# Latent attention: six key tiles transposed on TensorE in two groups of three, ten regrouped over DRAM

## Chip, cores and metric

One core of one Trainium2 chip runs the whole program. The metric is the device time of one execution in microseconds; less is better. Before the change it is 2612.72 us, the median of 3 runs (2611.89 to 2612.78).

## The reference

Four blocks follow one another on a [2048 tokens x 128] float32 array: a state-space block, a local-attention transformer, a latent attention, and a mixture of experts, with a layer norm between them. The change touches the third alone:

```python
h = layernorm(x) * ln_scale + ln_bias
c_q, c_kv = h @ w_down_q.T, h @ w_down_kv.T          # 64 latent channels each
q = rope(c_q @ w_up_q.T); k = rope(c_kv @ w_up_k.T)  # 16 heads of 64
v = c_kv @ w_up_v.T
attn = softmax(q @ k.T / 8)                          # 2048 x 2048 per head
out = (attn @ v) @ w_out.T + x
```

Attention isn't masked, so every head has 2048 x 2048 probabilities.

## The kernel before

**Tiling.** A unit of work is one head and one chunk of 512 queries; there are 64 of them (UNITS). Heads go in pairs (w = 0 and 1), and a pair of units (w = 0, then w = 1, on the same chunk j) is the period that repeats 32 times. A unit has four iterations, r = 0 to 3, one for each 128 queries; G = 4U + r counts them, 256 in all. The 2048 keys are 16 tiles of 128 (T).

**An iteration.** TensorE (L1597 to L1622) computes the scores of the *next* iteration, G + 1, into four PSUM banks of 512 keys (score_banks, L1377), banks 0 and 1 once the first half of the exponentials of G has left them, banks 2 and 3 after the second half. VectorE takes the row maximum of each bank and then of the four (row_max, L1407 to L1414). ScalarE turns the scores into probabilities in two halves of 1024 keys (exps, L1416 to L1422), into probs[:, slot] in SBUF, queries on partitions.

The product with the values needs keys on partitions, so the probabilities have to be turned, and this is done in two ways:

- Key tiles 0 to NEAR - 1 = 7 go through TensorE: turn_tiles (L1398) transposes four tiles of 128x128 into the one PSUM bank `turned`, and ScalarE copies the bank into `near` (copy_tiles, L1403). This happens twice in an iteration: group A (tiles 0 to 3) after the scores, then a stretch of the mix, then group B (tiles 4 to 7). ScalarE's order is copy A, both exps, copy B.
- Key tiles 8 to 15 (FAR = 8) go over DRAM: VectorE transposes 32x32 blocks of probs (turn_blocks, L1474 to L1480, 128x1024) into `blocks[:, r % 2]`, SP writes them to `bounce` in DRAM (write_blocks, L1482) and reads them back regrouped into `far[:, w]` (read_blocks, L1487).

turn_blocks(G) waits for the write of G - 2, which used the same half of `blocks` (L1477). It comes in VectorE's order after row_max(G + 1) and before row_max(G + 2); with r = 3 two small instructions for the softmax sums (reciprocals, L1466) stand between.

**The mix** of a unit's probabilities with the values (mix, L1424) comes one unit of the same head later, in pieces of four tiles: MIXED_AT (L1515) has tiles 4 to 7 in r = 0, 8 to 11 in r = 1, 12 to 15 in r = 2, and 0 to 3 of the other head's unit in r = 3. Before the first piece with a far tile TensorE waits until that head's four reads have landed (L1608). The first mixed result goes through the output matmuls in r = 0 (output, L1442). In the units with w = 0, r = 1 and r = 3 also project the next pair's queries and keys (pieces, L1384).

**SP's queue** is one list in a fixed order (L1524 to L1546). For a unit: wait for the head's earlier reads; write 0; (w = 1: send_keys, four transfers); write 1; wait for mix_done, which the mix of r = 2 sets (L1533), since `far[:, w]` is free only then; read 0; read 1; write 2; read 2, which waits for write 2 to land (L1488); write 3; (w = 0: send_keys); send_q, two transfers; read 3, which waits for write 3 to land. Then the next unit's write 0.

POOL adds outputs to the accumulator and makes the rotated keys and queries of the next pair (make_parts, L1492). It and SP are otherwise not touched.

Of the kernel before, what the change touches and what calls it, by code (L numbers as in the profile page):

```python
# [9 lines left out]
ACT = mybir.ActivationFunctionType  # L10
AX = mybir.AxisListType

P = 128
D = 128
S = 2048
T = S // P
CH = 512
# [1099 lines left out]
HEADS_G, HEAD_G, LATENT = 16, 64, 64  # L1117
# [3 lines left out]
RT = 4  # L1121
QH = QW // 2
HALVES = S // QH
NEAR = 8
FAR = T - NEAR
RUN = FAR * 32


def latent_attention(nc, dram, const, x, acc):

    ident = const["ident"]
    spare = x[:].rearrange("p t d -> p (t d)")
    values = spare[:, 0:T * LATENT].rearrange("p (t c) -> p t c", c=LATENT)
    raw = spare[:, T * LATENT:2 * T * LATENT].rearrange("p (k n) -> p k n", k=2)
    with Space(nc, "g") as sp:
        c = sp.sb("c", [P, S])
        waves = sp.sb("waves", [P, HALVES, 2, QH])
# [3 lines left out]
        with Space(nc, "ga") as s:  # L1141
            norm = s.sb("norm", [P, 2])
            w_down = s.sb("w_down", [P, 2 * LATENT])
            w_v = s.sb("w_v", [P, PAIRS_G, LATENT])
            w_o = s.sb("w_o", [P, PAIRS_G, D])
            hT = s.sb("hT", [P, S])
            turned = s.ps("turned", [P, 2, CH])
            down = s.ps("down", [P, 2, CH])
            v_ps = s.ps("v_ps", [P, 2, CH])
            m_ps = s.ps("m_ps", [P, 2, CH])  # L1150
            m = {n: s.sem(n) for n in ("loaded", "turn_done", "hT_ready", "down_done", "c_ready", "v_done", "m_done",
                                       "doubled", "copied")}
            with nc.Block() as block:

                @block.sync
                def _(sync):
                    for d, n in ((norm, "g_norm"), (w_down, "w_down"), (w_v, "w_v"), (w_o, "w_o")):
                        sync.dma_start(d[:], dram[n]).then_inc(m["loaded"], 16)
                    sync.dma_start(waves[:], dram["g_waves"]).then_inc(waves_loaded, 16)

                @block.tensor
                def _(pe):
                    for g in range(NC):
                        if g >= 2:
                            pe.wait_ge(m["hT_ready"], g - 1)
                        for k in range(4):
                            ins = nc.tensor.transpose(turned[:, g % 2, k * P:(k + 1) * P], acc[:, 4 * g + k], ident[:])
                        ins.then_inc(m["turn_done"], 1)
                    pe.wait_ge(m["loaded"], 4 * 16)
                    for c_ in range(NC):  # L1170
                        pe.wait_ge(m["hT_ready"], c_ + 1)
                        if c_ >= 2:
                            pe.wait_ge(m["c_ready"], c_ - 1)
                        nc.tensor.matmul(down[:, c_ % 2], w_down[:], hT[:, c_ * CH:(c_ + 1) * CH], start=True,
                                         stop=True).then_inc(m["down_done"], 1)
                    for t in range(T):
                        ins = nc.tensor.matmul(v_ps[:, t // 8, (t % 8) * LATENT:(t % 8 + 1) * LATENT],
                                               hT[:, t * P:(t + 1) * P], w_down[:, LATENT:], start=True, stop=True)
                    ins.then_inc(m["v_done"], 1)
                    for k in range(2):  # L1180
                        if k:
                            pe.wait_ge(m["copied"], 2)
                        for h in range(8 * k, 8 * k + 8):
                            rows = slice(h % 2 * 64, h % 2 * 64 + 64)
                            at = h // 2 % 4
                            for half in range(2):
                                ins = nc.tensor.matmul(m_ps[half * 64:half * 64 + 64, h % 2, at * P:(at + 1) * P],
                                                       w_v[rows, h // 2], w_o[rows, h // 2], start=True, stop=True)
                        ins.then_inc(m["m_done"], 1)

                @block.vector
                def _(dve):
                    dve.wait_ge(m["loaded"], 4 * 16)
                    for g in range(NC):
                        dve.wait_ge(m["turn_done"], g + 1)
                        nc.vector.tensor_scalar(hT[:, g * CH:(g + 1) * CH], turned[:, g % 2], norm[:, 0:1],
                                                norm[:, 1:2], ALU.mult, ALU.add).then_inc(m["hT_ready"], 1)

                    dve.wait_ge(m["turn_done"], NC)
                    nc.vector.tensor_scalar(acc[:], x[:], 2.0, None, ALU.mult).then_inc(m["doubled"], 1)  # L1200
                    for c_ in range(NC):
                        cols = slice(c_ * CH, (c_ + 1) * CH)
                        dve.wait_ge(m["down_done"], c_ + 1)
                        nc.vector.tensor_scalar(c[0:64, cols], down[0:64, c_ % 2], 0.125, None, ALU.mult)
                        nc.vector.tensor_copy(c[64:P, cols], down[64:P, c_ % 2]).then_inc(m["c_ready"], 1)
                    dve.wait_ge(m["v_done"], 1)
                    dve.wait_ge(m["doubled"], 1)
                    nc.vector.tensor_copy(values[:, 0:NEAR].rearrange("p t c -> p (t c)"), v_ps[:, 0])
                    nc.vector.tensor_copy(raw[:, 0], v_ps[:, 1])
                    by_head = mixers[:, 2:].rearrange("p (g h) n -> p h g n", h=2)  # L1210
                    for k in range(2):
                        dve.wait_ge(m["m_done"], k + 1)
                        for h in range(2):
                            nc.vector.tensor_copy(by_head[:, h, 4 * k:4 * k + 4],
                                                  m_ps[:, h].rearrange("p (g n) -> p g n", n=D)).then_inc(m["copied"], 1)

                @block.gpsimd
                def _(pool):
                    nc.gpsimd.memset(mixers[:, 0:2], 0.0)
# [6 lines left out]
        probs = sp.sb("probs", [P, 2, S])  # L1226
        near = sp.sb("near", [P, 2, NEAR, QW])
        far = sp.sb("far", [P, 2, RT * 4, FAR, 32])
# [10 lines left out]
        turned = sp.ps("turned", [P, CH])  # L1239
# [42 lines left out]
        with nc.Block() as block:  # L1282

            @block.sync
            def _(sync):
                load_w(sync, 0, 0)
                load_w(sync, 1, 1)
                for k in range(4):
                    sync.dma_start(values[k:P:4, NEAR:].rearrange("p t c -> p (t c)"), raw[32 * k:32 * k + 32, 0])\
                        .then_inc(m["values_set"], 16)  # L1290
                sync.wait_ge(m["values_set"], 64)
                sync.wait_ge(m["zeroed"], 1)
# [105 lines left out]
        def turn_tiles(pe, r, tiles):  # L1398
            for k, t in enumerate(tiles):
                ins = nc.tensor.transpose(turned[:, k * P:(k + 1) * P], probs[:, r % 2, t * P:(t + 1) * P], ident[:])  # L1400
            ins.then_inc(m["turn_done"], 1)

        def copy_tiles(act, w, r, tiles):  # L1403
            nc.scalar.activation(near[:, w, tiles, r * P:(r + 1) * P], turned[:].rearrange("p (t n) -> p t n", n=P),  # L1404
                                 ACT.Copy).then_inc(m["near_copied"], 1)

        def row_max(dve, slot, before):  # L1407

# [108 lines left out]
        with nc.Block() as block:  # L1517
# [55 lines left out]
            def _(pe):  # L1573
# [4 lines left out]
                with pe.Fori(0, PAIRS_G // 2) as i:  # L1578
                    for turn in range(2):
                        g = 2 * i + turn  # L1580
                        for j in range(NC):
                            for w in range(2):
                                U = 8 * g + 2 * j + w
                                for r in range(RT):
# [14 lines left out]
                                    pe.wait_ge(m["exp_done"], 2 * G + 2)  # L1599
                                    score_banks(pe, (2, 3), q, k_of)  # L1600
                                    pe.wait_ge(m["near_copied"], 2 * G + 1)
                                    turn_tiles(pe, r, range(0, 4))
                                    if r == 0:
                                        pe.wait_ge(m["piece_taken"], 2 * (8 * g + 2 * j) + (4 if w else 1))
                                        pe.wait_ge(m["mixed_ready"], U + 1)
                                        slot = 2 * (2 * i + turn + (j + 2 + w) // NC) + 1 - w
                                        output(pe, mixers[:, bass.ds(slot, 1)].rearrange("p a n -> p (a n)"))
                                    if r == 1:  # L1608
                                        pe.wait_ge(landed[w], 64 * (4 * g + j + 1))
                                    if r == 3:  # L1610
                                        pe.wait_ge(m["mixed_ready"], U + 2)
                                        pe.wait_ge(m["near_copied"], 8 * U + 1)
                                    mix(pe, w if r < 3 else 1 - w, MIXED_AT[r])
                                    pe.wait_ge(m["near_copied"], 2 * G + 2)
                                    turn_tiles(pe, r, range(4, 8))
                                    if w == 0 and r == 1:
                                        pe.wait_ge(w_loaded[1 - turn], 16 * (i + 1 + turn))
                                        pe.wait_ge(m["out_taken"], U + 1)
# [39 lines left out]
            def _(act):  # L1658
# [4 lines left out]
                with act.Fori(0, PAIRS_G // 2) as i:  # L1663
                    for turn in range(2):
                        g = 2 * i + turn
                        for j in range(NC):
                            for w in range(2):
                                U = 8 * g + 2 * j + w
                                H = 8 * g + 2 * j
                                for r in range(RT):  # L1670
# [12 lines left out]
                                            take_piece(act, H, 1)  # L1683
                                        act.wait_ge(m["recip_ready"], U + 3)
                                    act.wait_ge(m["turn_done"], 2 * G + 1)
                                    copy_tiles(act, w, r, slice(0, 4))
                                    act.wait_ge(m["blocks_turned"], G + 1)
                                    exps(act, (r + 1) % 2, w if r < RT - 1 else 1 - w, (r + 1) % RT, G + 2)
                                    if r == 0:
                                        act.wait_ge(m["near_read"], 2 * U + 2)  # L1690
                                    act.wait_ge(m["turn_done"], 2 * G + 2)
                                    copy_tiles(act, w, r, slice(4, 8))
                take_output(act, UNITS)
                take_mixed(act, UNITS + 1)
                take_output(act, UNITS + 1)
# [359 lines left out]
```

## Time and profile before

| what | value |
|---|---|
| time, median of 3 runs | 2612.72 us |
| the profiled execution's own time | 2612.52 us |
| its span | 2610.7 us |
| PE / PEld busy | 2243.0 us (86%) / 1316.3 us (50%) |
| DVE / ACT / POOL busy | 1667.3 us (64%) / 1356.4 us (52%) / 851.6 us (33%) |
| DMA moved | 350.10 MB, mean 134 GB/s |
| mean granted TensorE clock | 0.926 of full speed |

PE is TensorE's matmuls and PEld its weight loads, DVE is VectorE, ACT is ScalarE, POOL is GpSimd, SP issues transfers. The span runs from the first to the last instruction; the time of the execution has 1.8 us more around it. The main loop of the latent attention lies between about 1000 and 2391 us of the span. A line of the timeline gives start, duration, engine, line, operation, output and inputs, how many instructions are merged in it, and in brackets how long the engine sat idle before it and what released it. SPq marks transfers as SP issues them: their duration there is the issuing, not the transfer.

### The profile page before, as it was taken

What the parts mean: (1) busy time and instruction counts of PE and PEld (TensorE: products, weight loads), DVE (VectorE), ACT (ScalarE), POOL (GpSimd) and SP (SyncE); (2) the same over time, 40 slices, a digit from 0 to 9 for tenths busy, and PEclk for the clock granted to TensorE, in tenths of its full rate; (3) what the DMA queues carried; (4) which work ended last, traced back from release to release, by engine and by line L of the source; (5) the groups of instructions that cost most, each with busy time, mean ns of one, the idle gap of its engine ahead of it and who ended that gap; (6) DMA issues with size and microseconds to landing.
All of it is one profiled execution on the core that took longest, in us unless ns stands there. A gap on an engine that the chain in (4) does not pass through costs nothing. (4 is left out here: it accounts for less than half of the span.)

```text
span 2610.7 us, 38329 instructions
## 1 busy us (share of the span) xinstructions
PE 2243.0 (86%) x11694; PEld 1316.3 (50%) x11694; DVE 1667.3 (64%) x3060; ACT 1356.4 (52%) x2757; POOL 851.6 (33%) x868
## 2 busy tenths in 40 slices
PE   4737989389895548999999999999999999998297
PEld 2522358343484324555555555555555555554144
DVE  5863566435664556777767777677777677774544
ACT  4222345123453105777767777677777677775121
POOL 0712333113332023434344434344434344443000
PEclk8978989689898768999999999999999999999598
DMA  1002000000000045777767677767676777675000
GB/s 30 1 1 100 1 1 2 19 25 1 1 2 8 12 150 157 237 237 228 238 210 234 226 236 231 233 226 234 228 234 227 228 232 237 228 234 186 33 1 17
DMA packets 229184, 350.10 MB, mean 134 GB/s; under 512 B 21460, under 2 KB 173908, under 8 KB 228564
## 3 DMA queue, kind: packets, MB, share of 16 engines
q1 hardware_dynamic: 228948, 347.32, 40.8%
q8 instruction: 103, 1.69, 0.3%
q14 instruction: 133, 1.09, 0.1%
HBM read 151.96 MB, written 136.31 MB: 110 GB/s over the span
## 5 line engine op out<-in xcount | busy, mean ns | idle before, releaser
L1411 DVE TENSOR_REDUCE g.most<-g_score 128x1 f32<-128x512 f32 x1028 | 638.7, 683 | 341.9 <-PE g_score L1381 341.8
L1419 ACT ACTIVATE g.probs<-g_score,g.bias 128x1024 f32<-128x1024 f32 x514 | 568.1, 1110 | 69.6 <-DVE g.bias L1414 58.6
L1381 PE MATMUL g_score<-g.keys,g.q_unit 128*128 128x512 f32 x2056 | 560.6, 412 | 28.9 <-issue 12.5
L1404 ACT ACTIVATE g.near<-g_turned 128x512 f32<-128x512 f32 x512 | 305.4, 596 | 325.0 <-PE g_turned L1400 325.0
L1381 PEld LDWEIGHTS g_score<-g.keys,g.q_unit 128*128 128x128 f32 x2056 | 360.5, 190 | 148.7 <-ACT g.probs L1419 63.3
L1400 PEld LDWEIGHTS g_turned<-top.ident,g.probs 128*128 128x128 f32 x2048 | 234.2, 140 | 243.1 <-issue 208.1
L1478 DVE STREAM_TRANSPOSE g.blocks<-g.probs 128x1024 f32<-128x1024 f32 x256 | 318.8, 1245 | 37.2 <-DMA bounce<-g.blocks 24.3
L1400 PE MATMUL g_turned<-top.ident,g.probs 128*128 128x128 f32 x2048 | 321.7, 280 | 0.0
L1432 PE MATMUL g_mix_ps<-g.near,mid.y_tok 128*64 128x512 f32 x1056 | 258.8, 612 | 5.7 <-DMA g.far<-bounce 5.7
L1432 PE MATMUL g_mix_ps<-g.far,mid.y_tok 128*64 128x512 f32 x1056 | 255.2, 605 | 0.0
L1498 POOL TENSOR_TENSOR mid.y_tok<-mid.y_tok,g.waves 128x512 f32<-128x512 f32 x128 | 163.6, 1278 | 227.7 <-ACT mid.y_tok L1396 227.7
L1460 POOL TENSOR_TENSOR g.scaled<-g.scaled,g.recip 128x512 f32<-128x512 f32 x67 | 69.7, 1040 | 423.8 <-ACT g.scaled L1452 412.6
L1432 PEld LDWEIGHTS g_mix_ps<-g.near,mid.y_tok 128*64 128x64 f32 x1056 | 64.9, 138 | 104.1 <-issue 96.4
L1432 PEld LDWEIGHTS g_mix_ps<-g.far,mid.y_tok 128*64 128x64 f32 x1056 | 64.3, 136 | 99.8 <-issue 99.8
L1419 ACT ACTIVATION_READ_ACCUMULATOR g.probs<-g_score,g.bias 128x1 f32 x514 | 100.6, 196 | 0.0
L1501 POOL TENSOR_TENSOR mid.y_tok<-mid.y_tok 128x256 f32<-128x256 f32 x128 | 93.1, 727 | 10.1
L1509 POOL TENSOR_TENSOR g.k_part<-mid.y_tok,g.zero 128x256 fp32r<-128x256 f32 x64 | 39.2, 612 | 168.3 <-DMA g.keys<-g.k_part 163.0
L1464 POOL TENSOR_TENSOR top.x_tok<-top.x_tok,g.scaled 128x512 f32<-128x512 f32 x67 | 85.6, 1277 | 5.2
L728 POOL TENSOR_TENSOR la1.qkT<-lp1.rotated,lp1.turned_by 128x512 f32<-128x512 f32 x32 | 40.6, 1269 | 128.0 <-DVE lp1.turned_by L704 128.0
L728 POOL TENSOR_TENSOR la0.qkT<-lp0.rotated,lp0.turned_by 128x512 f32<-128x512 f32 x32 | 40.6, 1269 | 125.3 <-DVE lp0.turned_by L704 125.3
L1396 ACT ACTIVATE mid.y_tok<-g_side 128x512 f32<-128x512 f32 x128 | 77.4, 604 | 1.8
L1444 PE MATMUL g_side<-g.mixers,g.mixed 128*128 (+1 forms) x536 | 71.8, 278 | 1.2 <-ACT g.mixed L1440 1.2
(352 smaller groups left out, 3290.3 us busy)
## 6 DMA issues: line engine op xcount, KB each, us to landing
bounce<-g.blocks SPq DMA_DIRECT2D x256, 512.0 KB, 6.1
g.far<-bounce SPq DMA_DIRECT2D x256, 512.0 KB
g.q_unit<-g.q_pair SPq DMA_DIRECT2D x132, 256.0 KB, 4.7
g.keys<-g.k_part SPq DMA_DIRECT2D x256, 64.0 KB, 3.6
g.far<-g.near SPq DMA_DIRECT2D x8, 512.0 KB
lt.cos<-cos SPq DMA_DIRECT2D x1, 2048.0 KB, 8.1
lt.sin<-sin SPq DMA_DIRECT2D x1, 2048.0 KB, 12.2
g.waves<-g_waves SPq DMA_DIRECT2D x1, 2048.0 KB, 9.7
```

What stands on the lines that cost most here:

```text
L728: nc.gpsimd.tensor_tensor(qkT[:, f, cols(c)], rotated[:, n % 2], turned_by[:, n % 2], ALU.add)\
L1381: ins = nc.tensor.matmul(score[:, b], q[:, part], k_of(b), start=(part == 0), stop=(part == 1))
L1396: nc.scalar.activation(raw[:, kind], side[:, kind], ACT.Copy).then_inc(m["piece_taken"], 1)
L1400: ins = nc.tensor.transpose(turned[:, k * P:(k + 1) * P], probs[:, r % 2, t * P:(t + 1) * P], ident[:])
L1404: nc.scalar.activation(near[:, w, tiles, r * P:(r + 1) * P], turned[:].rearrange("p (t n) -> p t n", n=P), ACT.Copy).then_inc(m["near_copi ...
L1411: nc.vector.tensor_reduce(most[:, slot, k:k + 1], score[:, k], AX.X, ALU.max, negate=True)\
L1419: nc.scalar.activation(probs[:, slot, k * 2 * CH:(k + 1) * 2 * CH], score[:, 2 * k:2 * k + 2].rearrange("p b n -> p (b n)"), ACT.Exp, bias ...
L1432: ins = nc.tensor.matmul(out, values[:, t], moving, start=(t < 2), stop=(t >= T - 2))
L1464: nc.gpsimd.tensor_tensor(a, a, scaled[:], ALU.add).then_inc(m["added"], 1)
L1478: nc.vector.transpose(blocks[:, r % 2].rearrange("p j t c -> p t j c"), probs[:, r % 2, NEAR * P:].rearrange("p (t j a) -> p t j a", j=4, ...
L1498: nc.gpsimd.tensor_tensor(both, both, waves[:, at].rearrange("p s n -> p (s n)"), ALU.mult)\
L1501: nc.gpsimd.tensor_tensor(total, total, both[:, QH:], ALU.add).then_inc(m["order"], 1)
```

## The change

NEAR goes from 8 to 6, so FAR from 8 to 10. Group A is tiles 0 to 2 and group B tiles 3 to 5; the copy out of the PSUM bank has 384 columns. turn_blocks works on 128x1280, each write and read of `bounce` carries 640 KB for 512 KB, and a read's contiguous pieces (RUN * 4 bytes) are 1280 bytes for 1024, a write's 5120 for 4096. Tiles 6 and 7 are now far, and they are mixed in r = 0; the wait for the reads moves there from r = 1. The values of the ten far tiles are staged in one contiguous area by one copy more.

```diff
-NEAR = 8
+NEAR = 6
+TURN = NEAR // 2
 FAR = T - NEAR
 RUN = FAR * 32
...
+    spread_values = spare[:, T * LATENT:T * LATENT + FAR * LATENT]
...
-                    nc.vector.tensor_copy(values[:, 0:NEAR].rearrange("p t c -> p (t c)"), v_ps[:, 0])
-                    nc.vector.tensor_copy(raw[:, 0], v_ps[:, 1])
+                    nc.vector.tensor_copy(values[:, 0:NEAR].rearrange("p t c -> p (t c)"), v_ps[:, 0, 0:NEAR * LATENT])
+                    nc.vector.tensor_copy(spread_values[:, 0:CH - NEAR * LATENT], v_ps[:, 0, NEAR * LATENT:])
+                    nc.vector.tensor_copy(spread_values[:, CH - NEAR * LATENT:], v_ps[:, 1])
...
-                    sync.dma_start(values[k:P:4, NEAR:].rearrange("p t c -> p (t c)"), raw[32 * k:32 * k + 32, 0])\
+                    sync.dma_start(values[k:P:4, NEAR:].rearrange("p t c -> p (t c)"), spread_values[32 * k:32 * k + 32])\
...
-            nc.scalar.activation(near[:, w, tiles, r * P:(r + 1) * P], turned[:].rearrange("p (t n) -> p t n", n=P),
-                                 ACT.Copy).then_inc(m["near_copied"], 1)
+            nc.scalar.activation(near[:, w, tiles, r * P:(r + 1) * P],
+                                 turned[:, 0:TURN * P].rearrange("p (t n) -> p t n", n=P), ACT.Copy).then_inc(m["near_copied"], 1)
...
-                                    turn_tiles(pe, r, range(0, 4))
+                                    turn_tiles(pe, r, range(0, TURN))
                                     if r == 0:
...
                                         output(pe, mixers[:, bass.ds(slot, 1)].rearrange("p a n -> p (a n)"))
-                                    if r == 1:
                                         pe.wait_ge(landed[w], 64 * (4 * g + j + 1))
...
-                                    turn_tiles(pe, r, range(4, 8))
+                                    turn_tiles(pe, r, range(TURN, NEAR))
...
-                                    copy_tiles(act, w, r, slice(0, 4))
+                                    copy_tiles(act, w, r, slice(0, TURN))
...
-                                    copy_tiles(act, w, r, slice(4, 8))
+                                    copy_tiles(act, w, r, slice(TURN, NEAR))
```

## Rows read from the trace of the kernel before

**Rows 1.** Busy time by stretch; then waits, 1000 to 2400 (total us, times, longest).

```profile
core 0: us, PE busy (x) PEld busy (x) DVE busy (x) ACT busy (x) POOL busy (x), PEclk, DMA share, GB/s
1400.00:1500.00 100.00, 100.00 (x526) 59.14 (x523) 72.71 (x120) 73.79 (x133) 43.24 (x50) 1.00 0.70 232
...
DVE g.blocks L1478 <- DMA bounce<-g.blocks: 24.3, 30, 2.2
```

**Rows 2.** Groups of instructions, 1000 to 2400: count, busy us, mean ns, idle before.

```profile
L1400 PE MATMUL g_turned<-top.ident,g.probs 128*128 128x128 f32 x2044 | 321.1, 280 | 0.0
L1478 DVE STREAM_TRANSPOSE g.blocks<-g.probs 128x1024 f32<-128x1024 f32 x256 | 318.8, 1245 | 37.2 <-DMA bounce<-g.blocks 24.3 <-issue 4.5 <-ACT g.probs L1419 1.2
...
L1432 PE MATMUL g_mix_ps<-g.far,mid.y_tok 128*64 128x512 f32 x1040 | 251.6, 605 | 0.0
L1432 PE MATMUL g_mix_ps<-g.near,mid.y_tok 128*64 128x512 f32 x1032 | 249.9, 605 | 0.0
```

**Rows 3.** Timeline of PE, 1735 to 1785: the scores that open an iteration.

```profile
1739.17 2.25 PE L1381 MATMUL g_score<-g.keys,g.q_unit 128*128 128x512 f32 x8
1744.96 2.09 PE L1381 MATMUL g_score<-g.keys,g.q_unit 128*128 128x512 f32 x8
1750.94 2.12 PE L1381 MATMUL g_score<-g.keys,g.q_unit 128*128 128x512 f32 x8
1755.71 2.25 PE L1381 MATMUL g_score<-g.keys,g.q_unit 128*128 128x512 f32 x8
1761.84 2.11 PE L1381 MATMUL g_score<-g.keys,g.q_unit 128*128 128x512 f32 x8
1767.50 2.09 PE L1381 MATMUL g_score<-g.keys,g.q_unit 128*128 128x512 f32 x8
1772.24 2.25 PE L1381 MATMUL g_score<-g.keys,g.q_unit 128*128 128x512 f32 x8
1777.14 2.09 PE L1381 MATMUL g_score<-g.keys,g.q_unit 128*128 128x512 f32 x8
```

**Rows 4.** Timeline, 1766 to 1778: the rest of the iteration from 1767.50.

```profile
1768.23 2.48 DVE L1411 TENSOR_REDUCE g.most<-g_score 128x1 f32<-128x512 f32 x4 [1.66 <-PE g_score L1381]
...
1769.43 0.60 PE L1400 MATMUL g_turned<-top.ident,g.probs 128*128 128x128 f32 x4
...
1770.75 0.16 DVE L1414 TENSOR_REDUCE g.bias<-g.most 128x1 f32<-128x4 f32 x1
...
1770.94 1.11 ACT L1419 ACTIVATE g.probs<-g_score,g.bias 128x1024 f32<-128x1024 f32 x1 [0.28 <-DVE g.bias L1414]
...
1771.82 0.66 PE L1400 MATMUL g_turned<-top.ident,g.probs 128*128 128x128 f32 x4
```

**Rows 5.** SP's issues in a unit with w = 0, 1748 to 1790; then VectorE.

```profile
1755.50 0.93 SPq L1489 DMA_DIRECT2D g.far<-bounce  x2
1756.57 0.41 SPq L1484 DMA_DIRECT2D bounce<-g.blocks  x1
1762.83 0.36 SPq L1489 DMA_DIRECT2D g.far<-bounce  x1
1763.30 0.44 SPq L1484 DMA_DIRECT2D bounce<-g.blocks  x1
...
1768.43 0.66 SPq L1489 DMA_DIRECT2D g.far<-bounce  x1
1769.21 1.41 SPq L1484 DMA_DIRECT2D bounce<-g.blocks  x1
...
1776.15 1.25 DVE L1478 STREAM_TRANSPOSE g.blocks<-g.probs 128x1024 f32<-128x1024 f32 x1 [0.50 <-DMA bounce<-g.blocks]
```

**Rows 6.** Busy time by stretch: reads 0 and 1 moving, then write 2.

```profile
1758.00:1759.50 1.50, 1.50 (x10) 0.64 (x10) 1.09 (x4) 1.11 (x3) 1.25 (x1) 1.00 1.00 289
1760.00:1761.50 1.50, 1.50 (x12) 1.10 (x12) 0.74 (x1) 1.50 (x5) 1.26 (x3) 1.00 1.06 407
```

**Rows 7.** Timelines of DVE and PE, 2250 to 2270: the same wait, longest.

```profile
2255.99 1.25 DVE L1478 STREAM_TRANSPOSE g.blocks<-g.probs 128x1024 f32<-128x1024 f32 x1 [2.15 <-DMA bounce<-g.blocks]
...
2261.40 2.29 PE L1381 MATMUL g_score<-g.keys,g.q_unit 128*128 128x512 f32 x8 [1.09 <-ACT g.probs L1419]
```

## The prediction

> **What bounds the kernel now.** I read the busy time by stretch first. In the main loop TensorE is busy all the time at full granted clock, VectorE and ScalarE 73% and 74%, and the DMA engines 70% at 232 GB/s [rows 1]. By this alone TensorE is the limit, and taking work from it pays in full. The starts of the scores show that this holds in half of the iterations only [rows 3]. From one start to the next a pair of units has 5.79 (w = 0, r = 0), 5.98, 4.77, 6.13 (r = 1, 2, 3), 5.66, 4.74, 4.90 (w = 1, r = 0, 1, 2), and an r = 3 that is bare like the last two. Four are long: they hold the output matmuls or the projected pieces. Four are bare.
>
> A bare one is bound twice [rows 3, 4]. TensorE fills it, but there is also a loop through three engines: scores start at 1767.50, the first maximum 0.73 later (1768.23), four maxima take 2.48, the bias ends at 1770.91, the first half of the exponentials runs from 1770.94 to 1772.05, and the next scores start at 1772.24. That is 4.74 us with no gap over 0.3. TensorE's work in a bare iteration could vanish, and it would still take 4.74. The long ones have about an engine-microsecond to spare against this loop.
>
> Then the waits. The only stall by a transfer is VectorE's block transposition for the write two iterations before it: 30 times, 24.3 us in total, 0.81 on average [rows 1]. Rows 5 show where: in r = 2 of w = 1, once a pair. Its write (write 0 of w = 1) is issued at 1769.21, VectorE is ready at 1775.65, and starts at 1776.15 when it has landed, 6.9 after its issue. SP issued it that late because its queue is a chain: the mix of r = 2 (w = 0) and group B end before the scores of 1755.71 [rows 3], the mix itself at about 1755.3; reads 0 and 1 at 1755.50, write 2 at 1756.57, read 2 at 1762.83 when write 2 has landed, write 3 at 1763.30, read 3 at 1768.43 when write 3 has landed, write 0 at 1769.21 [rows 5]. The chain takes 20.9 us, VectorE is ready after 20.35. It is balanced to half a microsecond against compute, and the change lengthens it.
>
> **TensorE's part.** Two of eight transposes go. A group of four occupies 0.60 (A) and 0.66 (B) with a last one of 0.28 [rows 2, 4], so one more costs (0.60 - 0.28)/3 = 0.107 and (0.66 - 0.28)/3 = 0.127, together 0.234 an iteration. In the four long iterations that counts: 0.94. In the bare ones only what lies over the loop's 4.74: 4.77 and 4.90 give 0.03 and 0.15 less a rounding, 0.17. Sum 1.11 a pair, 32 pairs: **-35.5 us**. Bounds: 256 x 0.234 = 60 if the loop were no limit, 30 if only the long ones gain.
>
> **ScalarE's part.** Two copies an iteration lose a quarter of their columns. ScalarE is 26% idle [rows 1] and the copies stand before or after the exponentials, not in them, so I count nothing. If they were in the loop they would make it shorter, hence the 60 above.
>
> **VectorE's part.** The transposition goes from 1024 to 1280 columns: 1.245 us [rows 2] to 1.51 if some of it is fixed, 1.56 in proportion. It sits between the bias and the next maximum. In the tight place the bias ends at 1775.65 and the next maximum could start 0.73 after the scores of 1777.14, at 1777.87 [rows 3 to 5]: 2.22, less 1.25 and about 0.2 for the reciprocals, so a wait of about 0.8 is free there. The longest wait, 2.15, left TensorE idle for 1.09 and so had 0.8 to 1.06 free [rows 7]. With the longer transposition (0.27) and the loop at 4.75 for 4.90 (0.15) 0.4 is left. In itself the transposition costs nothing: VectorE's idle time covers it.
>
> **The mix.** Far and near matmuls take the same, 605 ns [rows 2], so tiles 6 and 7 cost the same from `far`. The wait for the reads comes one iteration earlier. Read 3 of a w = 0 unit goes out at 1768.43 [rows 5], the r = 0 mix that now needs it begins after 1782, the end of this pair [rows 3]. Even if it lands 2 us later than now there are some 6 us left: nothing, with the DMA queue backed up at most a few us.
>
> **The transfers.** Each of the 512 grows by 131 KB. The rates when the engines are full are 289 GB/s while reads move and 407 GB/s while a write does [rows 6], so +0.45 for a read and +0.32 for a write if all of it scales with bytes; if a read's packets have a fixed part, +0.3. In the chain from the end of the mix to the landing of write 0 stand reads 0 and 1 and write 2, read 2 and write 3, read 3 and write 0, each batch awaited: 4 x 0.45 + 3 x 0.32 = 2.8, or 7 x 0.3 = 2.1. I take 2.4, nearer the middle since the share is 1.00 to 1.06 in both stretches (the engines, not the issuing, are the limit), with a part of write 3's growth hidden by SP's own issuing of keys and queries. Lower bound 0 for the reads if their time is set by the count of packets, which stays: then 1.0. Page "DMA: Bandwidth & Descriptors" of the Trainium skill, section "Anatomy of one DMA", fits 2.0 us plus bytes / 436 GB/s (for another issuing path); by this estimate a transfer grows by 0.30 and the chain by 2.1, and the total below would come to 2650. This trace's reads are slower than that rate.
>
> At the same time compute gets to the place sooner: the mix of r = 2 ends 0.11 earlier in its iteration, but the long iterations r = 3 and r = 0 lose 0.23 each: VectorE is ready 20.0 after it for 20.35, 0.36 sooner.
>
> New wait: 0.7 now + 2.4 + 0.36 = 3.45 a pair, of which 0.4 is free, so 3.05 stall the loop of three engines. Nothing makes this good afterwards, as TensorE has no backlog. Today about 0.25 a pair is lost there (an average wait of 0.81 with 0.8 free, and a few long ones). Net 2.75. At the three back edges of the loop over pairs TensorE stands still anyway, so 29 pairs: **+80 us**. The opening copies, the larger fills and the last read that ends the stage: **+2**.
>
> Sum: -35.5 + 80 + 2 = +46 on the profiled execution's 2612.5, which is the median within 0.2: **2658 us**.
>
> **Rivals.**
> *A, the forecast: write 0 of w = 1 becomes the limit.* With growths of 2.1 to 2.8, 2648 to 2671; with doubts on the free part 2635 to 2685. For: 30 waits stand there already, in nearly every pair. Chance 0.64.
> *B, same place, cheap transfers.* If the chain grows by under 1.1, the stall is under 1.75 and gain and loss cancel: growth 1.0 gives 2616, growth 0 gives 2590. It decides at a growth of 0.8. Against: share 1.00 at only 289 GB/s. Chance 0.16.
> *C, faster: the wait doesn't bind.* Should SP's chain shrink elsewhere (issues of 0.66 and 1.41 at its end are partly the queue's backlog, and they might overlap the landing), the wait stays free, and TensorE's saving counts: 2612.5 - 36 = 2577; with a shorter loop too, 2553. "Perfetto Trace Analysis" of the Trainium skill, section "Identifying the Most-Contended Engine", says to optimise first the engine with the highest occupancy, here TensorE; by that rule it is this case. The busy share speaks for it, the 4.74 loop and the waits against. It needs a chain that grows by next to nothing, since the free 0.4 is less than today's wait. Chance 0.13.
> *D, worse: more places wait.* The engines' share goes from 0.70 to about 0.84. If writes 2 and 3 come late for the next unit's r = 0 and r = 1 too, or the reads for the mix, a second stall of 1 to 2 us a pair adds 30 to 60: 2690 to 2720. Chance 0.07.
> That the change does not do what it says would show in the counts; nothing in it is conditional.
>
> **Chances and range.** About 0.2% (5 us) is what a measurement of this kernel tells from no change. Faster: C and half of B, 0.21. Same: the other half of B, 0.08. Slower: 0.71. A's own range is 2635 to 2685. For 8 in 10 the range has to take in B and the lower end of D: 2586 to 2694.
>
> **What would show it.** Right: L1400 has 1536 matmuls; the block transposition takes 1.5 us; read 2 is issued 7.1 to 7.5 after write 2 instead of 6.3; VectorE waits about 3.4 us for `bounce` in some 30 places, 100 us in all, in r = 2 of w = 1; that bare r = 3 iteration grows to 7.5 to 8; long iterations are 0.23 shorter, the other bare ones 4.75; DMA share about 0.8. Wrong: a DVE wait total under 40 us (B or C), bare iterations under 4.7 (the loop was no limit), or idle time of TensorE before the mix of r = 0 (D).

## The result, and the profile after

The changed kernel takes **2765.85 us** (2761.06 to 2771.67, 4 runs) against 2612.3 us (2608.01 to 2612.78) of the kernel before: ratio 1.0593, 95% interval 1.0564 to 1.0621. It is slower by 153 us. The forecast said slower by 46, with 2694 as its upper end.

The page, with the lines that answer to [rows 1, 2], first whole-span busy times, then the costliest groups (line engine op, out<-in, shapes, count | busy, mean ns | idle before, releaser):

```profile
span 2759.6 us, 37306 instructions
PE 2274.7 (82%) x11182; PEld 1312.4 (48%) x11182; DVE 1735.8 (63%) x3061; ACT 1296.9 (47%) x2757; POOL 850.1 (31%) x868
...
L1481 DVE STREAM_TRANSPOSE g.blocks<-g.probs 128x1280 f32<-128x1280 f32 x256 | 387.0, 1512 | 203.4 <-DMA bounce<-g.blocks 187.1
...
L1403 PE MATMUL g_turned<-top.ident,g.probs 128*128 128x128 f32 x1536 | 273.2, 288 | 22.4 <-ACT g.near L1407 22.4
```

The work did what was foreseen: 1536 transposes for 2048, VectorE's transposition 1.512 us. The time went into a wait: VectorE for the writes to `bounce`, 187.1 us for 24.3 [rows 1]. Who waited for whom (total us, times, longest), 1000 to 2550:

```profile
DVE g.blocks L1481 <- DMA bounce<-g.blocks: 187.1, 91, 5.3
...
ACT g.near L1407 <- DVE g.recip L1475: 71.7, 26, 3.7
...
PE g_score L1384 <- DMA g.keys<-g.k_part: 29.9, 8, 5.0
```

The second line is new, and the third as good as new (0.2 us before). With r = 3, ScalarE waits for the reciprocals before copy A, and those now stand behind the late transposition; and TensorE waits 8 times for the keys of the next pair of heads, whose transfers come behind write 0 in SP's queue.

The same place as in [rows 5], SP's issues of one unit with w = 0, and VectorE at its end:

```profile
1835.59 2.22 SPq L1492 DMA_DIRECT2D g.far<-bounce  x2
1837.94 0.41 SPq L1487 DMA_DIRECT2D bounce<-g.blocks  x1
1845.30 0.36 SPq L1492 DMA_DIRECT2D g.far<-bounce  x1
1845.77 0.44 SPq L1487 DMA_DIRECT2D bounce<-g.blocks  x1
...
1851.73 0.43 SPq L1492 DMA_DIRECT2D g.far<-bounce  x1
1852.29 1.62 SPq L1487 DMA_DIRECT2D bounce<-g.blocks  x1
...
1860.28 1.51 DVE L1481 STREAM_TRANSPOSE g.blocks<-g.probs 128x1280 f32<-128x1280 f32 x1 [4.41 <-DMA bounce<-g.blocks]
```

From read 0 to VectorE's start on the landing of write 0 it is 24.7 us, for 20.65 (1755.50 to 1776.15). Link by link against [rows 5]: reads 0 and 1 to write 2, 2.35 for 1.07 (SP itself takes 2.22 to issue the two reads, for 0.93); landing of write 2, 7.36 for 6.26; of write 3, 5.96 for 5.13; read 3 to write 0, 0.56 for 0.78; landing of write 0, 7.99 for 6.94. This unit lies above the mean: over 31 pairs the way from read 0 to VectorE's start takes 24.31 us on average for 20.85, and VectorE is ready for it after 20.08 for 20.16.

What TensorE makes of it, the starts of the scores as in [rows 3]:

```profile
1851.98 2.29 PE L1384 MATMUL g_score<-g.keys,g.q_unit 128*128 128x512 f32 x8
1857.17 2.31 PE L1384 MATMUL g_score<-g.keys,g.q_unit 128*128 128x512 f32 x8 [0.23 <-ACT g.probs L1422]
1865.96 3.63 PE L1384 MATMUL g_score<-g.keys,g.q_unit 128*128 128x512 f32 x8 [2.71 <-ACT g.probs L1422]
1872.92 2.10 PE L1384 MATMUL g_score<-g.keys,g.q_unit 128*128 128x512 f32 x8
```

r = 3 of w = 1 takes 8.79 us (1857.17 to 1865.96), and the next iteration, which doesn't wait for any transfer, 6.96. Its scores take 3.63 us for 2.10. Busy time by stretch says why (PE, PEld, DVE, ACT, POOL, granted clock, DMA share, GB/s):

```profile
1857.20:1866.00 8.80, 5.05 (x23) 2.54 (x23) 5.63 (x9) 3.67 (x8) 3.27 (x4) 0.99 0.89 288
1865.90:1869.40 3.50, 3.44 (x8) 2.73 (x9) 2.15 (x4) 1.49 (x4) 0.00 (x0) 0.51 0.70 269
```

TensorE was busy for 5.05 of 8.80 us, and then the granted clock is 0.51, the lower of its two levels (1.2 of 2.4 GHz).

The account over 31 pairs, from the starts of the scores, mean us before and after:

| iteration | before | after | forecast |
|---|---|---|---|
| w = 0: r = 1, 2, 3 | 5.98, 4.77, 6.14 | 5.76, 4.74, 6.00 | 5.75, 4.75, 5.90 |
| w = 1: r = 0, 1 | 5.66, 4.74 | 5.45, 4.72 | 5.43, 4.75 |
| w = 1: r = 2 | 4.93 | 5.89 | 4.75 |
| w = 1: r = 3 | 5.40 | 8.50 | 7.97 |
| w = 0: r = 0 (next pair) | 5.96 | 6.98 | 5.72 |

(The last two hold the three back edges of the loop in both kernels, so their forecast is the value before plus 80/31, and the value before less 0.23.) The 31 pairs take 1489.2 us for 1350.9, 138 more; the start and the last units another 11 (span less the pairs, 1270.4 for 1259.8). That is the profiled execution, 2761.43 us.

### The profile page after: what moved, and what is told of

It reads as the page before. It is cut to its first block and busy times, and to the rows that moved or that the text cites. A ratio compares the mean times of both kernels' runs of the same rounds, so it can differ in the third digit from the quotient of the medians.

```text
span 2759.6 us, 37306 instructions
## 1 busy us (share of the span) xinstructions
PE 2274.7 (82%) x11182; PEld 1312.4 (48%) x11182; DVE 1735.8 (63%) x3061; ACT 1296.9 (47%) x2757; POOL 850.1 (31%) x868
## 5 line engine op out<-in xcount | busy, mean ns | idle before, releaser
L1384 PE MATMUL g_score<-g.keys,g.q_unit 128*128 128x512 f32 x2056 | 607.3, 438 | 125.9 <-ACT g.probs L1422 73.9
L1384 PEld LDWEIGHTS g_score<-g.keys,g.q_unit 128*128 128x128 f32 x2056 | 388.7, 203 | 273.4 <-ACT g.probs L1422 146.4
L1481 DVE STREAM_TRANSPOSE g.blocks<-g.probs 128x1280 f32<-128x1280 f32 x256 | 387.0, 1512 | 203.4 <-DMA bounce<-g.blocks 187.1
L1407 ACT ACTIVATE g.near<-g_turned 128x384 f32<-128x384 f32 x512 | 250.9, 490 | 435.2 <-PE g_turned L1403 362.9
L1435 PE MATMUL g_mix_ps<-g.far,mid.y_tok 128*64 128x512 f32 x1320 | 322.7, 602 | 0.0
L1403 PEld LDWEIGHTS g_turned<-top.ident,g.probs 128*128 128x128 f32 x1536 | 185.5, 144 | 270.8 <-issue 193.5
L1403 PE MATMUL g_turned<-top.ident,g.probs 128*128 128x128 f32 x1536 | 273.2, 288 | 22.4 <-ACT g.near L1407 22.4
L1435 PE MATMUL g_mix_ps<-g.near,mid.y_tok 128*64 128x512 f32 x792 | 204.8, 625 | 6.2 <-DMA g.far<-bounce 6.2
L1435 PEld LDWEIGHTS g_mix_ps<-g.far,mid.y_tok 128*64 128x64 f32 x1320 | 83.4, 136 | 136.7 <-issue 136.7
L1435 PEld LDWEIGHTS g_mix_ps<-g.near,mid.y_tok 128*64 128x64 f32 x792 | 46.9, 140 | 69.5 <-issue 61.9
```

What stands on the lines that cost most here:

```text
L1384: ins = nc.tensor.matmul(score[:, b], q[:, part], k_of(b), start=(part == 0), stop=(part == 1))
L1435: ins = nc.tensor.matmul(out, values[:, t], moving, start=(t < 2), stop=(t >= T - 2))
L1481: nc.vector.transpose(blocks[:, r % 2].rearrange("p j t c -> p t j c"), probs[:, r % 2, NEAR * P:].rearrange("p (t j a) -> p t j a", j=4, ...
```

## The experiments

A line number in a trace's row is that of the run's own kernel. Each ratio is to the kernel before as it ran beside that experiment: 2612.87 us for 1 to 4, 2613.3 for 5 to 8, 2616.7 for 9 to 11.

**1. The bytes taken back.** All instructions of the change, with 512 KB a transfer: the last 256 of each partition's 1280 elements aren't moved, so two far tiles hold stale numbers.

```diff
-                           blocks[:, r % 2].rearrange("p j t c -> p (j t c)")).then_inc(written[r % 2], 16)
+                           blocks[:, r % 2].rearrange("p j t c -> p (j t c)")[:, 0:4 * SHORT]).then_inc(written[r % 2], 16)
...
-            sync.dma_start(far[:, w, 4 * r:4 * r + 4].rearrange("p i t c -> p i (t c)"),
+            sync.dma_start(far[:, w, 4 * r:4 * r + 4, 0:8].rearrange("p i t c -> p i (t c)"),
```

> The changed kernel, but every write and read of bounce carries 512 KB as before (the last 256 of each partition's 1280 elements stay behind, so two of the ten far tiles keep stale numbers). All its instructions stay. Theory (the extra bytes in SP's chain are the whole loss): 2612.5 - 36 = about 2577 (2570 to 2585), the DVE wait for bounce falls from 187 us to under 40, iterations r = 3 (w = 1) and r = 0 (w = 0) go from 8.8 and 7.0 to 4.8 and 5.6. Rival (the longer transposition on VectorE, or the wait for the reads moved to r = 0, is part of the loss): over 2600, with a wait for bounce that is small but r = 3 still over 6.

Measured 2597.93 us (2593.16 to 2604.04), ratio 0.9935 (0.9918 to 0.9951). The bytes are worth 2766 - 2598 = **168 us**, more than the whole loss, and the rest of the change, longer transposition and earlier wait for the reads among it, is a gain of 15. It isn't the 36 expected: the time lies between the expected range and the rival's. The wait doesn't vanish:

```profile
DVE g.blocks L1482 <- DMA bounce<-g.blocks: 36.3, 34, 4.2
```

That is my own sum: with the same chain, VectorE is ready 0.36 us sooner and has 0.4 free for 0.8, so the wait of 0.7 grows to 1.06 and 0.66 of it stalls, 29 x 0.66 = 19 us less the 7 lost before, 12. The trace has r = 3 of w = 1 at 5.80 us for 5.40, 12 us in 31 pairs. The expectation had left this out; the prediction had it. The other 9 us stay open.

**2. ScalarE's second wait.** The wait for the reciprocals moved behind copy A.

```diff
                                             take_piece(act, H, 1)
-                                        act.wait_ge(m["recip_ready"], U + 3)
                                     act.wait_ge(m["turn_done"], 2 * G + 1)
                                     copy_tiles(act, w, r, slice(0, TURN))
+                                    if r == 3:
+                                        act.wait_ge(m["recip_ready"], U + 3)
```

> The changed kernel, but ScalarE waits for the reciprocals in r = 3 after copy A instead of before it. The changed kernel's trace shows ScalarE waiting 72 us there, 26 times, since the reciprocals stand behind the late block transposition on VectorE. Theory (the exponentials still wait for the maxima behind the same transposition, so copy A has time): ScalarE's wait for the reciprocals disappears, the time stays within 6 us of the changed kernel's 2766, at most 15 less. Rival (this second coupling adds to the stall): 40 to 70 us less.

Measured 2782.47 us (2774.74 to 2794.61), ratio 1.0663 (1.0635 to 1.0690), above the range of both. The wait is gone from the trace, and nothing is gained; the rival is out. That it is some 17 us slower wasn't expected; the trace shows more waiting for `bounce` (204.6 us up to 2400), but why stays open.

**3. TensorE kept busy.** 8 extra transposes of the identity before group B and 20 after it, w = 1, r = 3 only.

```diff
+                                    if w == 1 and r == 3:
+                                        pe.wait_ge(m["piece_taken"], 2 * (8 * g + 2 * j) + 5)
+                                        filler(pe, 8)
                                     pe.wait_ge(m["near_copied"], 2 * G + 2)
                                     turn_tiles(pe, r, range(TURN, NEAR))
+                                    if w == 1 and r == 3:
+                                        filler(pe, 20)
```

> The changed kernel, with 28 extra transposes of a constant tile into a free half bank in r = 3 of w = 1, 8 before group B and 20 after it, about 3 us of TensorE work in its idle time there. Theory (after some 3 us of idling TensorE is granted the lower clock, and the next scores take 3.6 us for 2.1): scores in r = 0 of w = 0 take 2.1 to 2.3 again and that iteration goes from 7.0 to 5.5, 27 pairs x 1.5 = 40 us less, 2726 (2715 to 2745). Rival (the long scores come from something else, such as the load of the transfers): no gain, and up to 20 us more from the extra work.

Measured 2800.59 us (2796.83 to 2803.16), ratio 1.0715 (1.0697 to 1.0733): 35 more, not 40 less. The mechanism did what the theory said: r = 0 of w = 0 went from 6.98 to 5.55 us on average. But what VectorE waits for `bounce` rose, and the waits are in other iterations now:

```profile
1847.71 1.51 DVE L1485 STREAM_TRANSPOSE g.blocks<-g.probs 128x1280 f32<-128x1280 f32 x1 [3.25 <-DMA bounce<-g.blocks]
1854.19 1.51 DVE L1485 STREAM_TRANSPOSE g.blocks<-g.probs 128x1280 f32<-128x1280 f32 x1 [2.41 <-DMA bounce<-g.blocks]
```

These are r = 1 and r = 2 of a unit with w = 0; all waits of VectorE for `bounce` come to 265.1 us up to 2400. On average over 31 pairs r = 2 and 3 of w = 0 went from 4.74 and 6.00 to 5.14 and 7.18 us, r = 0 of w = 1 from 5.45 to 5.89. I read this as a row of awaited transfers that closes on itself: write 0 lands, VectorE transposes, write 2 goes out, lands, read 2, write 3, read 3, the next unit's write 0. At 640 KB it limits the units with w = 0 too, as soon as compute gets through them quicker. r = 3 of w = 1 grew as well, from 8.50 to 9.03, though VectorE's wait at its place hardly did (138.8 us in all for 135.7); why stays open. Whether the clock costs anything in total had to be asked where the transfers have slack: experiments 9 and 10.

**4 and 5. SP's order.** The bytes stay, the order changes: write 2 goes ahead of the wait for the mix and of reads 0 and 1, write 3 ahead of read 2. Then write 2 alone.

```diff
                                 write_blocks(sync, w, 1, G + 1)
+                                write_blocks(sync, w, 2, G + 2)
                                 sync.wait_ge(m["mix_done"], U + 1)
...
-                                write_blocks(sync, w, 2, G + 2)
+                                write_blocks(sync, w, 3, G + 3)
                                 read_blocks(sync, w, 2, G + 2)
-                                write_blocks(sync, w, 3, G + 3)
```

> The changed kernel with SP's queue in another order: write 2 ahead of the wait for the mix and of reads 0 and 1, write 3 ahead of read 2. The bytes are the same. Theory (not the bytes by themselves but the row of awaited landings in SP's queue makes the loss: mix, reads, write 2, read 2, write 3, read 3, write 0): write 0 of w = 1 goes out some 4 us earlier, the DVE wait for bounce falls under 30 us, and only TensorE's saving is left: 2612.5 - 36 - 7 = about 2571 (2562 to 2590). Rival (the DMA engines are too full at 640 KB, about 0.85 of them busy, whatever the order): over 2680, with the waits moved to other places.

Measured 2588.89 us (2582.58 to 2592.46), ratio 0.9904 (0.9884 to 0.9923), within the theory's range.

> The changed kernel with write 2 alone moved ahead of the mix's wait and of reads 0 and 1; write 3 stays behind read 2. Theory (the longest link is write 2 queued behind 1280 KB of reads, landing 7 us after its issue; alone it lands in 3.4): read 2 goes out at 6 us after the mix for 8.6 now, write 0 some 2.5 to 3 us earlier, most of the wait of 4.2 goes: 2600 to 2630. Rival (write 3 behind read 2 keeps the chain long and the gain is small): over 2700.

In this one write 3 stays behind read 2. Measured 2586.97 us (2581.92 to 2588.26), ratio 0.9891 (0.9875 to 0.9908), better than expected: one moved write removes the whole loss, with all the bytes in place. So the bytes cost what they do because SP's order makes them wait for one another, not because the engines are full; in the second version the engines are busier, 0.84 at 282 GB/s for 0.79 at 250 in the changed kernel, and VectorE hardly waits for them:

```profile
1000.00:2350.00 1350.00, 1332.37 (x6593) 756.54 (x6591) 1074.12 (x1644) 933.17 (x1771) 570.13 (x632) 0.99 0.84 282
```

```profile
DVE g.blocks L1481 <- DMA bounce<-g.blocks: 8.9, 13, 1.1
```

SP's queue in it:

```profile
1404.77 0.32 SPq L1487 DMA_DIRECT2D bounce<-g.blocks  x1
1405.33 3.25 SPq L1492 DMA_DIRECT2D g.far<-bounce  x3
1409.48 0.34 SPq L1487 DMA_DIRECT2D bounce<-g.blocks  x1
```

Read 2, which waits for write 2 to land, goes out with reads 0 and 1, all three within 3.25 us, and write 3 follows 4.7 us after write 2 for the 7.8 (1837.94 to 1845.77) of the changed kernel.

**6. The order alone.** The kernel before, eight near tiles, with the order of experiment 4.

> The kernel before (eight near tiles, 512 KB) with SP's queue in the order of the last run: write 2 ahead of the mix's wait and the reads, write 3 ahead of read 2. Theory (the order pays only where VectorE waits for bounce beyond its free time, some 7 us in all before the change, and six near tiles are worth the rest of what that run gained): 2606 (2600 to 2610), 15 to 20 above the reordered change's 2589. Rival (the order alone is worth the whole gain and six near tiles are worth nothing): 2585 to 2592.

Measured 2602.24 us (2596.92 to 2608.58), ratio 0.9961 (0.9946 to 0.9975), within the theory's range; no wait of VectorE for `bounce` is left in its trace. The order is worth some 10 us by itself, and with this same order (experiment 4) six near tiles are worth 2602 - 2589 = 13 more.

**7 and 8. Reads or writes.** The changed kernel with only the writes, then only the reads, at 512 KB (stale numbers in two far tiles as in 1).

> The changed kernel with reads of 640 KB and writes of 512 KB (each partition's last 256 elements aren't written, so the far tiles get stale numbers; four extra fills before the loop). In SP's chain up to the landing of write 0 stand four reads and three writes. All the extra bytes cost 2766 - 2598 = 168 us. Theory (every byte in the chain counts, reads at the slower rate of 289 against 407 GB/s, 4 x 0.45 against 3 x 0.32 us): reads are two thirds of it, 2598 + 110 = about 2708 (2685 to 2725). Rival (only the awaited writes' own length and landing matter): under 2650.

> The changed kernel with writes of 640 KB and reads of 512 KB (256 of 320 elements of each piece are read back, so two of the ten far tiles stay stale). Theory: the writes' third of the loss, 2598 + 58 = about 2656 (2640 to 2680). Rival (only the awaited writes matter): over 2700.

Measured 2719.56 us (2718.37 to 2729.26), ratio 1.0415 (1.0392 to 1.0438), with long reads; 2674.52 us (2665.04 to 2690.32), ratio 1.0243 (1.0199 to 1.0288), with long writes. Over the 2598 of experiment 1 that is 122 for the reads and 77 for the writes, both in their ranges, 61 to 39. Both count, the reads more, as their number in the chain and their rate [rows 6] say. Their sum, 198, is over 168, so they don't add up simply; the last of these times varies by 25 us from run to run.

**9 and 10. The wait without the transfers.** On the version of experiment 5, a reduction of 3.88 us over constants on VectorE in place of the wait; then the same with the extra transposes of experiment 3.

```diff
+                                    if w == 1 and r == 2:
+                                        nc.vector.tensor_reduce(pad[:], waves[:, 0:7].rearrange("p h s n -> p (h s n)"),
+                                                                AX.X, ALU.max)
                                     turn_blocks(dve, r, G)
```

> The version with write 2 first (2587), whose transfers hardly make VectorE wait, with one reduction over constants put on VectorE ahead of the block transposition in r = 2 of w = 1, about 3.8 us, once a pair. It stands for the wait of 4.2 us that the changed kernel has there, without any load on the transfers. Theory (the stall costs its length less some 0.4 free, and after it TensorE's next scores run at the lower granted clock, 1.5 us more in r = 0 of w = 0): 3.4 + 1.5 in 29 pairs, 2587 + 142 = about 2729 (2710 to 2745), scores of r = 0 take 3.6 us. Rival (the lower clock comes from the load of the transfers or from nothing to do with the idle time): 3.4 x 29, 2587 + 99 = about 2686, scores of r = 0 at 2.1 to 2.3.

> The same, with the 28 extra transposes in r = 3 of w = 1 (8 before group B, 20 after it, some 3 us of TensorE work in its idle time). In the changed kernel they brought the scores of the next iteration back to full clock, but no time, as waits for the transfers grew in the units with w = 0. Theory (there the row of awaited transfers took the time back; here it has slack, so the clock's part comes back in the total): 29 x 1.4 less than the run without them, about 2688 (2670 to 2705). Rival (keeping TensorE busy costs what it gives): 2720 or more.

Measured 2737.39 us (2732.61 to 2740.94), ratio 1.0470 (1.0446 to 1.0495), and 2684.78 us (2682.22 to 2686.97), ratio 1.0271 (1.0251 to 1.0291). With VectorE waiting for no transfer there the picture of the changed kernel comes back, idle time and slow scores:

```profile
1424.69 3.78 PE L1385 MATMUL g_score<-g.keys,g.q_unit 128*128 128x512 f32 x8 [2.71 <-ACT g.probs L1423]
1428.27 0.84 PE L1404 MATMUL g_turned<-top.ident,g.probs 128*128 128x128 f32 x3
```

The iteration before and these scores by stretch, as above:

```profile
1416.60:1424.70 8.10, 5.04 (x26) 2.54 (x23) 8.01 (x10) 3.67 (x8) 0.76 (x2) 0.95 0.44 140
1424.70:1428.40 3.70, 3.70 (x9) 2.82 (x10) 2.30 (x4) 1.41 (x3) 0.00 (x0) 0.50 1.04 338
```

With the filler (the reduction still there) TensorE goes on at full speed, and the granted clock of these scores is 1.00, with the DMA engines as full as in the stretch above (a share of 1.03):

```profile
1408.99 2.35 PE L1409 MATMUL g_side<-top.ident 128*128 128x128 f32 x20
1411.42 2.29 PE L1385 MATMUL g_score<-g.keys,g.q_unit 128*128 128x512 f32 x8
```

So 3.9 us a pair in VectorE's way cost 2737 - 2587 = 150 us, and 53 of these are the clock: on average r = 0 of w = 0 takes 7.61 us without the filler and 5.72 with it, r = 3 of w = 1 8.39 and 8.47. Both times are in their theory's range, and both rivals are out.

**11. Further on.** Experiment 5 with NEAR = 4 and groups of two, 768 KB a transfer.

> The version with write 2 first, with four near tiles and twelve over DRAM (768 KB a transfer). Theory (with the order mended the next limit is the transfers' own volume: the engines are 0.87 busy at 282 GB/s, and 768 KB ask for about 337 GB/s at the present pace, over the 324 that a share of 1.0 gives): a pair takes at least 43.6 us for 41.3, so 2640 to 2690, with VectorE waiting for bounce again. Rival (TensorE's saving goes on, 0.9 us a pair less 0.3 for the longer transposition): 2567 (2560 to 2580).

Measured 2708.51 us (2704.13 to 2709.72), ratio 1.0355 (1.0333 to 1.0376), 18 over the theory's range and far from the rival's. The engines' share is 0.89 at 303 GB/s, and VectorE waits 134.4 us for `bounce` in 1000 to 2350:

```profile
1000.00:2350.00 1350.00, 1222.51 (x5582) 672.69 (x5581) 1043.72 (x1512) 804.06 (x1628) 521.36 (x580) 0.96 0.89 303
```

That isn't the volume by itself, which would be a share of 1.0. The expectation had the share too high besides: 0.87 is that of experiment 4, and experiment 5's 0.84 puts a share of 1.0 at 336 GB/s, about what 768 KB ask for. That the chain is too long again is how I read the waits; no experiment tried it. The granted clock of 0.96, for 0.99 in experiment 5, goes with slow stretches behind the stalls, as in the changed kernel.

## Why the prediction was right and where it was wrong

*TensorE's part: right.* 0.234 us from each long iteration, nothing from the bare ones but what lay over the three-engine loop. The table has 5.76 and 5.45 where 5.75 and 5.43 were worked out, and 4.72 to 4.74 where 4.75 was; the bare iterations never went under the loop. Half the iterations were bound by the loop, and one place by a wait. The Trainium skill, "Perfetto Trace Analysis", section "Identifying the Most-Contended Engine", says to optimise first the engine with the highest occupancy, but to judge TensorE's headroom by its matmul FLOPs against the peak and by the busy share of its weight loads, not by how busy its matmuls are. The prediction took the matmuls' 100% and left this out; the weight loads have 59% [rows 1], less than VectorE's 73% and ScalarE's 74%. Neither share shows the loop or the wait.

*VectorE, the mix, the moved wait: right within 9 us.* Experiment 1 has all of them, and is faster than before; they weren't tried one by one.

*The place of the wait and its direction: right.* Write 0 of w = 1, in r = 2: 135.7 of the 187.1 us that VectorE waits for `bounce` stand there. The mechanism is forecast A's. Its ground was a little weaker than told: 24 of the 30 waits before were at this place, not all. And rival B's 2616 for a growth of 1.0 comes to 2620 by the prediction's own terms.

*The transfers: mis-sized.* The term "I take 2.4" for the growth of the chain measured 3.5 on average over 31 pairs (24.31 for 20.85) and 4.0 in the unit above, and the average wait there is 135.7 us in 32 pairs, 4.24, for 3.45. Two things were missing. The three awaited landings grew by 0.97, 0.47 and 1.81 us on average (1.10, 0.83 and 1.05 in the unit above), 3.25 together, where 2.4 were taken for everything. And SP's issue of the two reads went from 1.01 to 1.66 us on average (0.93 to 2.22 in the unit above), a link that was priced at nothing; read 3 to write 0 took 0.4 less. The other term of the wait was too high: VectorE was to be ready 0.36 us sooner, and was 0.08 sooner. The estimate from the Trainium skill, "DMA: Bandwidth & Descriptors", section "Anatomy of one DMA", 0.30 a transfer and 2.1 for the chain, was further off (its fit is for transfers issued by GpSimd): landings of 640 KB took more than 0.30 longer here in all three places.

*"Nothing makes this good afterwards, as TensorE has no backlog": the step that failed.* It priced a stall at its own length. What follows a stall of this length costs too, since TensorE then runs at the lower clock: r = 0 of w = 0 took 6.98 for 5.72, 1.26 x 31 = 39 us. Experiments 9 and 10 show it without a wait for transfers, 53 us there. In the changed kernel itself these 39 us say where the time stands, not what could be had back: in experiment 3 they went, and the total rose. The trace of before had it already, away from the place of the change. At the first back edge the same scores come after 4.89 us of idle time, at a granted clock of 0.50:

```profile
1345.77 3.77 PE L1381 MATMUL g_score<-g.keys,g.q_unit 128*128 128x512 f32 x8 [4.89 <-issue]
```

At the end of the stage TensorE waits 5.69 us for a read, and the 16 mix matmuls after it take 6.58 us, the next 16 3.61.

*What else waits: missed.* The keys of the next pair of heads come behind write 0, and the transpositions of w = 1, r = 1 wait in 18 pairs (18.3 us). Both lengthen r = 2 of w = 1, 5.89 for 4.75, 1.14 x 31 = 35 us. Rival D had the idea (a second stall, 30 to 60 us) with a chance of 0.07. It belonged to A: once a chain is the limit in one place, it has no slack left for the places behind it.

The longer wait itself, (8.50 - 7.97) x 31 = 16, then 39 and 35, 3 in r = 3 of w = 0 (6.00 for 5.90) and 9 at the ends of the stage (11 for 2) come to 102, for the 103 us between 2658 and the profiled execution's 2761.4. By this account the longer wait and the small terms alone come to 28 us over the forecast, within its range; the clock and the other waits took it out.

## What to carry to other kernels

Before moving work from a busy engine to a queue, follow one queue through a period and add up its awaited landings: where the chain is within a microsecond of compute, added bytes cost time though the engines have room on average (168 us here, at a mean share of 0.70 before and 0.79 after). Then look at the order: a write that others wait for belongs ahead of reads that nobody needs yet, and here one such move turned a loss of 5.9% into a gain of 1.1% (2586.97 us). And price a stall of a few microseconds on TensorE with the slow stretch behind it, which was a third of the loss in experiment 9.

## What the runs showed of the hardware

- Idle time of TensorE cost more than its length. After 8.80 us with TensorE busy for 5.05, its granted clock was 0.51 and the scores took 3.63 us for 2.10; with the idle time filled with transposes (experiment 10) they took 2.29.
- SP's issue time isn't fixed. Two reads of 640 KB took 2.22 us to issue in one unit (1.66 on average), two of 512 KB 0.93 in another (1.01); three of 640 KB took 3.25.
- A two-input VectorE instruction on 128x4 elements has a median of 0.121 us, and up to 0.68. In the slow case shown, from the run of experiment 4, it begins while GpSimd runs and ends as GpSimd ends:

```profile
1204.57 0.74 POOL L1514 TENSOR_TENSOR g.q_pair<-mid.y_tok,g.q_pair 128x256 fp32r<-128x256 f32 x1
1204.66 0.67 DVE L1472 TENSOR_TENSOR g.recip<-g.sums 128x4 f32<-128x4 f32 x1
```

Of the 65 such instructions of that run 19 take over 0.2 us. Each of the 19 begins while a GpSimd instruction runs and ends 0.016 to 0.023 us after that one ends, and none is slow where GpSimd begins after it. It stands ahead of the maxima of r = 3, w = 1, an iteration that takes 4.99 us in the median there, for 4.73 of the other bare ones. That VectorE waits there for GpSimd to end is the reading that fits; no experiment changed one of the two alone.
